# Attention loop: the weighted sum of a score tile runs three tiles behind its scores, with four probability buffers instead of three

## What is computed

```python
q = apply_rotary(rmsnorm(q), cos, sin)
k = apply_rotary(rmsnorm(k), cos, sin)
scores = jnp.einsum('bhqd,bhkd->bhqk', q, k)          # q already times 1/sqrt(hd)
scores = jnp.where(causal[None, None], scores, -jnp.inf)
attn = jax.nn.softmax(scores.astype(jnp.float32), axis=-1)
attn = attn[:, :, 0] - lam * attn[:, :, 1]
out = jnp.einsum('bhqk,bhkd->bhqd', attn, v)
out = layernorm(out) * (1.0 - LAMBDA_INIT)
```

## Time and profile before

| what | value |
|---|---|
| runs shown | 7265.27 and 7776.11 us, median 7520.69 us |
| profiled execution | 7265.42 us |
| its span, slowest core (core 2) | 7263.9 us |
| spans of the 8 cores | 7250.4 to 7263.9 us |
| mean granted TensorE clock | 0.81 on every core |
| TensorE matmul, weight load | 4802.1 us (66%), 2712.6 us (37%) |
| VectorE, ScalarE, GpSimd | 2316.8, 1571.2, 309.5 us |

### The profile page before, as it was taken

How to read it: one execution, slowest core, us unless ns; L and a number is a source line. 1 busy time by engine, 2 the same in 40 slices (tenths; PEclk the granted TensorE clock), 3 DMA queues, 4 the chain that set the end, 5 groups by cost and what they waited for, 6 DMA issues and landing times. The chain is left out here.

```text
span 7263.9 us, 83779 instructions; the slowest of 8 cores (7250.4 to 7263.9 us)
## 1 busy us (share of the span) xinstructions
PE 4802.1 (66%) x28532; PEld 2712.6 (37%) x28532; DVE 2316.8 (32%) x5627; ACT 1571.2 (22%) x3639; POOL 309.5 (4%) x368
## 2 busy tenths in 40 slices
PE   3244398987989879889893555536555465546549
PEld 0011143433434334334343444425444344434434
DVE  1400322131221312212114345454443454444440
ACT  1244201101001011010110144203440143203431
POOL 0000001101001010010110000000000000000001
PEclk9566598988989989899996777767777787767779
DMA  4133114314143142350430000000000000000005
GB/s 99 68 134 136 56 23 71 47 35 76 23 65 47 35 76 30 58 64 20 80 47 12 6 6 5 10 12 4 5 12 7 7 5 6 9 12 4 5 33 89
DMA packets 193109, 279.21 MB, mean 38 GB/s; under 512 B 12083, under 2 KB 130996, under 8 KB 182452
## 3 DMA queue, kind: packets, MB, share of 16 engines
q0 software_dynamic: 51984, 100.72, 11.5%
q1 hardware_dynamic: 140708, 173.14, 7.7%
HBM read 173.05 MB, written 109.05 MB: 39 GB/s over the span
## 5 line engine op out<-in xcount | busy, mean ns | idle before, releaser
L1553 PE MATMUL avps<-vth,pbh 128*128 128x132 bf16 x2304 | 545.6, 252 | 748.6 <-DVE pbl L1769 541.1
L1769 DVE TENSOR_TENSOR pbl<-p,pbh 128x256 bf16<-128x256 f32 x1152 | 486.4, 425 | 627.8 <-PE sps L1532 291.2
L1003 PE MATMUL gps<-xnh,gslb 128*128 128x512 bf16 x1280 | 494.6, 386 | 221.1 <-DVE uslb L959 221.1
L1553 PEld LDWEIGHTS avps<-vth,pbh 128*128 128x128 bf16 x2304 | 260.5, 113 | 907.2 <-issue 867.4
L1559 PE MATMUL avps<-vtl,pbh 128*128 128x132 bf16 x2304 | 550.7, 254 | 0.0
L1565 PE MATMUL avps<-vth,pbl 128*128 128x132 bf16 x2304 | 549.6, 254 | 0.0
L1234 PE MATMUL sps<-wslb,xnh 128*128 128x256 bf16 x1536 | 430.8, 280 | 175.4 <-DVE wslb L1216 175.4
L1066 PE MATMUL yps<-auh,dslb 128*128 128x512 bf16 x1280 | 492.0, 384 | 31.2 <-PEq L898 31.2
L1008 PE MATMUL gps<-xnl,gslb 128*128 128x512 bf16 x1280 | 494.3, 386 | 0.0
L1013 PE MATMUL gps<-xnh,gslb 128*128 128x512 bf16 x1280 | 493.3, 385 | 0.0
L1070 PE MATMUL yps<-aul,dslb 128*128 128x512 bf16 x1280 | 491.8, 384 | 0.0
(11 more groups left out here) (254 smaller groups left out, 7767.3 us busy)
## 6 DMA issues: line engine op xcount, KB each, us to landing
out<-ybuf POOLq DMA_DIRECT2D x320, 256.0 KB, 5.3
xtile<-xT SPq DMA_DIRECT2D x64, 1024.0 KB, 4.7
dsl<-edwT SPq DMA_DIRECT2D x8, 2048.0 KB, 9.0
gsl<-egwT SPq DMA_DIRECT2D x32, 512.0 KB, 3.9
usl<-euwT SPq DMA_DIRECT2D x32, 512.0 KB, 5.2
xloc<-xT SPq DMA_DIRECT2D x8, 1024.0 KB
out<-xT POOLq DMA_DIRECT2D x1, 8192.0 KB, 79.1
otb<-otd SPq DMA_DIRECT2D x8, 1024.0 KB, 8.5
```

The costliest lines, as they stand in the source:

```text
L1003: t.matmul(gps[it % 2][:, :], gslb[ic % 2][:, 0, cci, :], xnh[:, cci, sl], start=(cci == 0), stop=False).then_inc(TE.h, 1)
L1553: t.matmul(pav[:, 0:132], pbh[(i - 2) % 3][:, ssl], vth[:, hl, kc, 0:132], start=(kc == 0), stop=False).then_inc(TE.h, 1)
L1769: v.tensor_tensor(pbl[i % 3][:, :], p32[i % 3][:, :], pbh[i % 3][:, :], AL.subtract).then_inc(VE.h, 1)
```

## The change

The order on TensorE is written with AV three items behind S; `p32`, `pbh` and `pbl` become four tiles each and are indexed by i % 4; exp(i) and split(i) wait for AV(i-4). The `sps` tiles stay three, and S(i) still waits for exp(i-3). AV(0) of a group waits for `rcp1` and `t11` of the group before, that is for the readers of `avps[0..1]`, and the first AV of the second map waits for `stt1`. The tables are counted anew. The queues of ScalarE and VectorE keep their order.

```diff
-    p32 = [sb(f"p32{i}", [128, 256], cx=ax) for i in range(3)]
-    pbh = [sb(f"pbh{i}", [128, 256], BF16, cx=ax) for i in range(3)]
-    pbl = [sb(f"pbl{i}", [128, 256], BF16, cx=ax) for i in range(3)]
+    p32 = [sb(f"p32{i}", [128, 256], cx=ax) for i in range(4)]
+    pbh = [sb(f"pbh{i}", [128, 256], BF16, cx=ax) for i in range(4)]
+    pbl = [sb(f"pbl{i}", [128, 256], BF16, cx=ax) for i in range(4)]
...
-                        for i in range(n + 2):
+                        for i in range(n + 3):
...
-                            if i >= 2:
-                                cp, kc = items[i - 2]
-                                t.wait_ge(VE.h, ve_p[(qt, i - 2)])
-                                if kc == 0 and qt >= 1 and cp == 0:
-                                    t.wait_ge(VE.h, ve_stt2[qt - 1])
+                            if i >= 3:
+                                cp, kc = items[i - 3]
+                                t.wait_ge(VE.h, ve_p[(qt, i - 3)])
+                                if kc == 0 and qt >= 1:
+                                    if cp == 0:
+                                        t.wait_ge(VE.h,
+                                                  ve_evac[qt - 1]["rcp1"])
+                                        t.wait_ge(SE.h,
+                                                  se_evac[qt - 1]["t11"])
+                                    else:
+                                        t.wait_ge(VE.h, ve_stt2[qt - 1])
...
-                                             pbh[(i - 2) % 3][:, ssl],
+                                             pbh[(i - 3) % 4][:, ssl],
...
-                        if i >= 3:
-                            s.wait_ge(TE.h, te_after_av[(qt, i - 3)])
+                        if i >= 4:
+                            s.wait_ge(TE.h, te_after_av[(qt, i - 4)])
```

More of the change, by code:

```diff
@@ L1437, in build_program @@
                             te_after_s[(qt, i)] = tcnt
-                        if i >= 2:
+                        if i >= 3:
                             tcnt += 6
-                            te_after_av[(qt, i - 2)] = tcnt
+                            te_after_av[(qt, i - 3)] = tcnt
                     te_group[qt] = tcnt
@@ L1565, in f_t @@
                                     t.matmul(pav[:, 0:132],
-                                             pbl[(i - 2) % 3][:, ssl],
+                                             pbl[(i - 3) % 4][:, ssl],
                                              vth[:, hl, kc, 0:132],
@@ L1635, in expi @@
                                                    len(qt_items[qt - 1])
-                                                   - 3 + i)])
+                                                   - 4 + i)])
                         if kc >= 2 * qt:
-                            s.activation(p32[i % 3][:, :], sps[i % 3][:, 0:256],
+                            s.activation(p32[i % 4][:, :], sps[i % 3][:, 0:256],
                                          AF.Exp).then_inc(SE.h, 1)
                         else:
-                            s.activation(p32[i % 3][:, :], sps[i % 3][:, 0:256],
+                            s.activation(p32[i % 4][:, :], sps[i % 3][:, 0:256],
                                          AF.Exp)
-                            s.activation(pbh[i % 3][:, :], sps[i % 3][:, 0:256],
+                            s.activation(pbh[i % 4][:, :], sps[i % 3][:, 0:256],
                                          AF.Exp).then_inc(SE.h, 1)
@@ L1753, in spliti @@
                         v.wait_ge(SE.h, se_exp[(qt, i)])
-                        if i >= 3:
-                            v.wait_ge(TE.h, te_after_av[(qt, i - 3)])
+                        if i >= 4:
+                            v.wait_ge(TE.h, te_after_av[(qt, i - 4)])
                         elif qt >= 1:
@@ L1759, in spliti @@
                                                    len(qt_items[qt - 1])
-                                                   - 3 + i)])
+                                                   - 4 + i)])
                         if kc >= 2 * qt:
                             msk = m0 if kc == 2 * qt else m1
-                            v.tensor_tensor(p32[i % 3][:, :],
-                                            p32[i % 3][:, :],
+                            v.tensor_tensor(p32[i % 4][:, :],
+                                            p32[i % 4][:, :],
                                             msk[:, :], AL.mult)
                             v.drain()
-                            v.tensor_copy(pbh[i % 3][:, :], p32[i % 3][:, :])
+                            v.tensor_copy(pbh[i % 4][:, :], p32[i % 4][:, :])
                             v.drain()
-                        v.tensor_tensor(pbl[i % 3][:, :], p32[i % 3][:, :],
-                                        pbh[i % 3][:, :], AL.subtract
+                        v.tensor_tensor(pbl[i % 4][:, :], p32[i % 4][:, :],
+                                        pbh[i % 4][:, :], AL.subtract
                                         ).then_inc(VE.h, 1)
```

## The result

| | before | after |
|---|---|---|
| lowest time | 7262.3 us | 7048.1 us |
| profiled execution (span) | 7265.42 (7263.9) | 7051.99 (7050.4) |
| sum of the eight attention blocks, core 2 | 1868.4 | 1646.6 |
| mean granted clock, all cores | 0.81 | 0.82 |

The ratio of after to before is 0.9705, with an interval of 0.9692 to 0.9719: 2.95% faster. The forecast, 7060 against 7265.42, is a ratio of 0.9717. Some executions of every version, before and after, run up to 10% longer, with a lower clock on part of the cores; they are left out of the times here, so that some versions have only one or two, and one of them is the 7776.11 that lifts the median shown before to 7520.69.

What follows compares the result with a forecast made beforehand. The attention blocks were taken as bound by a chain of waits, with no engine full and a low clock half the time. Terms 90 + 29 + 49 + 26 + 12 = 206 us off 7265 gave 7060, 8-in-10 range 6985 to 7150.

Steps and rivals of the forecast that it cites:

- Term 1: Group start: AV(0) comes 0.47 us earlier and part B about 1.6 us earlier per group, 90 us in all.
- Term 5: Clock at group starts: a shorter hole may keep it high, 0 to 50 us, taken as 12.
- I take a quarter: Clock at group starts: of at most 50 us, 12 were counted, as no row shows what such a hole does.
- Term 2: Restart behind exp(6): S(9) no longer waits for AV(6), all that follows comes 0.60 us earlier, 29 us.
- from there TensorE is full, so all that follows comes 0.60 earlier: Restart, from S(9) on: 0.60 us saved in each of groups 2 to 7, 29 us in eight blocks.
- Terms 3 and 4: Loop at the high clock: waits beyond TensorE's pace go, 49 us; masked items get one more item of cover, 26 us.
- the waits of AV for `oc` vanish: Group start in the changed trace: AV waits for the activation L1595 instead, about 2.4 us, 56 times.
- Rival 1: Loop and masked items: waits return as S waiting for exp or through ScalarE; 119 us gained, 7145; chance 0.11.
- Rival 3: Part B: split(5) is bound by exp(3) behind part A, so the gap stays; 101 us gained, 7165; chance 0.09.
- Rival 4: After restarts the clock never rises again, so the kernel gets slower: +126 us, 7390; chance 0.03.
- Rival 2: Group starts: the clock stays high, worth 50 us instead of 12; 244 us gained, 7020; chance 0.14.

Runs made afterwards that it cites:

- x_start: Kernel before with four buffers and the new AV(0) wait; AV three items behind S only up to AV(5), then two: 7169 and 7170 us, ratio 0.9869.
- x_wait: Kernel before with one edit, AV(0) waits for rcp1 and t11 instead of stt1: 7236.6 us, ratio 0.9959.
- x_stt: Changed kernel with the old wait, AV(0) waiting for stt1 again: 7077 and 7079 us, ratio 0.9743.
- x_tail: Four buffers, old AV(0) wait, AV three items behind S only from AV(7) on, two before: 7176 and 7179 us, ratio 0.9863.
- x_afl2: Kernel before (lead of two, three buffers, old wait) with part A moved ahead of item 0: 7061 to 7062 us, 7123 profiled, ratio 0.9724.
- x_afirst: Changed kernel with part A ahead of item 0 instead of item 3: 6915 and 6918 us, ratio 0.9504.

## Where the prediction was right, and where not

- **Basis.** The terms summed to 206 us and the profiled execution is 213 shorter. The number stood against the profiled execution, 7265.42, and not against the median of the two runs shown, 7520.69; against that median the same 7060 would be a gain of 6.1%, double the 2.95% measured.
- **Term 1, group start, and Term 5, clock.** Forecast 90 + 12 = 102. x_start, which has these alone, measured 102 in its trace; the changed kernel 122. AV(0)'s part was sized right: 26 forecast, 28.7 from S(0) to AV(0), 28 and 25 in time (x_wait, x_stt). The missing 20 us are put down to the clock: groups 4 to 7 take 14.17 us from S(0) to exp(6) after and 14.73 in x_start, 0.56 x 32 = 18. In x_start 7 of 56 groups do AV(0) to AV(2) at the high clock (in under 1.5 us), in the changed kernel 19, before none. The 19 starts at the high clock came to exp(6) 2.8 us earlier than before, the other 37 only 1.8. So this is the largest miss of the sum: term 5 stood at 12 us, and with term 1 at its 90 it measured 32. The step that failed is "I take a quarter": the clock was taken as if it hung on the hole alone, while the same holes with the loop's waits gone ahead of them kept the clock more often. No run separates term 5 from term 1 by itself.
- **Term 2, restart.** The other step that failed: "from there TensorE is full, so all that follows comes 0.60 earlier". Forecast 29, measured 16. S(9) did come 1.2 us sooner, and S(10) 0.61 sooner than in x_tail, but the clock rose at the same time as there.
- **Terms 3 and 4, loop and masked items.** Forecast 75 from one block's count, measured 82 (x_tail's trace) and 88 in time. In block 3 no step between unmasked items behind the restart is longer than 0.70; at the masked items in the middle of group 7 steps of 0.96 and 1.20 are left. The end of a group stayed at 3.83, as said.
- **Errors of opposite sign.** The measured terms, 122, 16 and 82, sum to 220 in the blocks of the trace, 14 more than forecast, while the errors taken one by one, 20, 13 and 7, come to 40; 8 us were then given back outside the blocks. The number was better than its terms: that it came within 8 us is in part luck.
- **Readings.** Part B takes 6.31 us by the rows (5397.74 to 5404.05), not 6.4; no term uses it. And of the 40 groups "3 to 7, whose S(0) starts at the high clock" 34 did so in the trace before.
- **Signs named beforehand.** S(0) to AV(0) 4.4: measured 4.36 in the group shown, 4.37 as the median of all. S(9) 0.80 behind exp(6): measured 0.80. The block 208 to 210 us: 206.1. S(0) to exp(6) 14.8: 14.3 on average in groups 3 to 7. The sign that failed is "the waits of AV for `oc` vanish": the profile still shows 52 of 56. The wait did move, as the end times show and x_wait and x_stt measure; the name of the releaser did not.
- **Rivals.** Rival 1 (only the gap moves) falls with x_tail, 88 us without the group start and the restart. Rival 3 (the gap does not move) falls with exp(6), which came 2.2 us earlier. Rival 4 (the low clock stays) falls with the mean clock of the blocks, not lower than before. Rival 2 (the clock stays high at group starts) came true in 19 of 56 groups.

The rule of the Trainium skill weighed for term 5 (TensorE: Matmul & The Clock Gate, Why this matters for your kernels), that long idle gaps send the clock down, agrees with the direction: before, with holes of 3.2 to 4.5 us, no group start stayed high; in x_afl2 and x_afirst, whose holes there are shorter than 2 us, 42 and 43 of 56 did. Read as a line drawn by the hole's length, it does not sort the 39 holes of 2.43 us in the changed kernel: behind 15 the clock held, behind 24 it did not. There the measurement decides.

## What to carry to other kernels

Count a software pipeline's lead against the longest chain that runs past it, and ask separately what the queues of the other engines do with small side work: where that work stands was worth nearly as much here as one item of lead (7061 against 7053) and costs no memory. Cut a chain that passes to and fro between two engines at every hand-over and put an item in each cut; cutting it once only makes a second hole. Time won in a stretch at the low clock counted for about half here (16 us of 29), where the clock's rise did not move with it.

## What was not expected of the hardware

Holes of the same length are followed by different clocks, and the clock falls mostly behind the hole, not in it. Two group starts of the changed kernel, both in block 3, come after matmuls at the high clock and a hole of 2.43 us. Group 7, in the section on the result, went on at 0.22 us (AV) and 0.27 us (S). Group 3 did not:

```profile
5171.28 0.24 PE L1559 MATMUL avps<-vth,pbh 128*128 128x132 bf16 x1 [2.43 <-DVE oc L1701]
5171.53 0.32 PE L1559 MATMUL avps<-vth,pbh 128*128 128x132 bf16 x1
5171.86 0.42 PE L1532 MATMUL sps<-qEh,kpkh 128*128 128x256 bf16 x1
```

The granted clock is 1.00 through both holes. In group 3 it is 0.50 from 0.06 us after the start of AV(0), in group 7 it holds for 8.5 us, into the next long stop. Of the 40 starts of groups 3 to 7 the clock had fallen ahead of AV(0) in 6; in 24 it fell within 1.4 us after AV(0) began, in 10 it held for 8 us or more.

Of the 19 group starts that stayed high 17 lie in groups 4 to 7, which follow the longer groups, and x_start, with holes of the same size but with the waits in the loop still there, has 7. What the engine did before the hole thus seems to bear on what comes after it; no run here changes that alone.
